# Gates' sums of the slot attention in pairs of token tiles, and a new table for the program's order

## The chip, the cores and the metric

The kernel runs on one core of a Trainium2 chip. The metric is the device time of one execution in microseconds (us), the median of several runs; lower is better.

## What is computed

Two sequences of 512 tokens, 128 features wide, pass through four layers. Each layer adds a gated attention on a context of 77 tokens and then a gated feed-forward part: (0) 16-head attention and a dense MLP, (1) multi-query attention and a mixture of 16 experts with two chosen and a shared expert, (2) attention and 32 experts with one chosen, (3) slot attention with a GRU cell, and an int8 matrix product. The part that the change touches is the slot attention of layer 3, three rounds of:

```python
for _ in range(3):
    sn = rmsnorm(slots, slot_norm_w)
    q = sn @ Wq.T
    attn = softmax(q @ k_proj.T * scale, axis=slots)      # over the 512 tokens
    attn = attn / (attn.sum(over the 77 keys) + EPS)
    updates = attn @ v_proj
    # GRU cell
    r = sigmoid(ir + hr);  z = sigmoid(iz + hz);  n = tanh(inn + r * hn)
    slots = (1 - z) * n + z * slots
```

Here (ir, iz, inn) comes from the updates through the input weights, (hr, hz, hn) from the slots through the hidden weights, each 3 x 128 wide.

## The kernel before

**Tiles.** The two sequences are called halves, h0 and h1 (`b` in the code). A half's 512 tokens are T = 4 tiles of 128 tokens. All activations stay on the chip.

**The order of the program.** The work is cut into steps named (phase, arguments). One step may have a piece on the matrix engine (PE), ScalarE (ACT), VectorE (DVE) and GpSimd (POOL). `half_steps` lists the steps of a half with a cost for each engine's piece and what it comes after; `schedule()` picks the steps one by one with a list scheduler whose ranks are shifted by the numbers in the table `LATER` (tenths of us, one for each piece of each half, and of the common preparations). What comes out is `ORDERS`, an order for each engine, in which that engine issues its instructions; engines wait for each other by semaphores. `schedule()` also deals the 8 PSUM banks and puts filler matmuls (128x512 on constants, their result is not read) where it expects PE to be idle.

**A round of slot attention** (`it` = 0, 1, 2) in a half:
- `square`: ACT squares and sums the slots (L1516, four ACTIVATEs), POOL makes the reciprocal root (L947, L948).
- `slots_turn`: PE transposes the slots (L1307), ACT copies them out of PSUM (L1382, tile q).
- `slot_products`: PE makes key products (8 matmuls), DVE scales them by the reciprocal root (L1843).
- `slot_scores`: PE transposes the products (L1332), DVE takes each key's maximum over the tokens (L1849), ACT the exponential (L1526).
- `hidden` 0, 1, 2: PE multiplies the slots by the hidden weights; ACT copies 0 and 1 (L1531), DVE scales and biases 2 (L1856).
- `slot_inverse`: DVE takes a reciprocal (L1865) and scales the values with it (L1866).
- `gru` 0 to 3: for each token tile PE makes one 386-column product into a bank of its own; DVE takes the reciprocal of its last column (L1877), and then multiplies by it and adds the hidden part (L1878, 384 columns, here called a tile's sum). The sum reads the reciprocal that DVE has just written, so `link` lets DVE wait for its own semaphore between the two: a hand-over.
- `gru_r`, `gru_z`, `gru_end`: ACT's tanh of the gates (L1537, L1541, L1542, L1547) and DVE's four products and sums of 512 columns and the product for z (L1884, L1885; L1890; L1894, L1895). After `gru_end` the slots are new.

After round 2: `slots_back` (L1901), and then for stage 7 `norm` (L1575, L1578, POOL L918), `norm_end` (L1584), `integers` (L1594 to L1596), `rounded` (L1602), PE's `turn` (L1074), its eviction (ACT L1382, DVE L1911), and `quantised`.

Of the rest, this is needed below: in the mixture of experts of layer 1, `gate` k and `up` k are pairs of products; ACT evicts a gate with Silu, DVE multiplies it with up. `gates1` is the choice of experts: DVE computes (L1757 to L1767), ACT takes an exponential and a tanh (L1487, L1488), and `weights_turn` continues on DVE (L1774 on).

```python
        step("gru", it, t, ... pe=0.65, dve=0.73)
    step("gru_r", it, after=[at("dve", "gru", it, T - 1)], act=0.53, dve=1.33)
```

Of the kernel before, what the change touches and what calls it, by code (L numbers as in the profile page):

```python
# [7 lines left out]
ALU = mybir.AluOpType  # L8
# [10 lines left out]
D = 128  # L19
# [122 lines left out]
def first_columns(name, k):  # L142
# [133 lines left out]
def half_steps(b, step):  # L276
# [108 lines left out]
    for it in range(ITERS):  # L385
# [13 lines left out]
        for t in range(T):  # L399
            step("gru", it, t, after=[at("dve", "slot_inverse", it)] + in_order("pe", "gru", it, t),  # L400
                 then={"dve": [at("act", "hidden", it, 1), at("dve", "hidden", it, 2)] + in_order("dve", "gru", it, t)},
                 pe=0.65, dve=0.73)
# [109 lines left out]
def units_of(phase, b, args):  # L512
# [37 lines left out]
    if phase in one:  # L550
        name, reader = one[phase]
        return [((name, *args[:1], b, *args[1:]), reader)]
    return {"project": [(("out", *args[:1], b), "dve")],
            "quantised": [(("out", 7, b), "dve")]}.get(phase, [])


def before_end(name):

    return BY_LANE[name[0]] * (LANES - 1 - name[-1]) if name[0] in BY_LANE else 0.0


def finished_by(phase, b, args):
# [11 lines left out]
    if phase == "choose":  # L574
        return units_of("hidden2", b, args)
# [1464 lines left out]
```

## Time and profile before

| | |
|---|---|
| median of 3 runs | 319.64 us (319.19 to 319.65) |
| the profiled execution's own time | 319.92 us |
| its span, first to last instruction | 318.1 us |
| PE busy | 301.1 us, 95% |
| DVE busy | 230.1 us, 72% |
| ACT busy | 144.1 us, 45% |
| POOL busy | 60.0 us, 19% |
| granted PE clock, mean | 0.999 |

The time outside the span is 319.92 - 318.1 = 1.8 us. Fillers count as busy PE. Busy times are sums over the whole program, whose parts have different limits; the rows below show the parts.

### The profile page before, as it was taken

Reading aid. Unit: us, or ns where it says so; the run is one execution under the profiler, and the core shown is the slowest. Engines: PE = TensorE matmul, PEld = TensorE weight load, DVE = VectorE, ACT = ScalarE, POOL = GpSimd, SP = SyncE. Lnnn points to the kernel's source line nnn. Section 1 sums busy time; section 2 is a strip of 40 time slices with the busy share of each in tenths; the row PEclk is TensorE's granted clock in tenths of the full one; section 3 lists DMA queues with packets and bytes.
Section 4 is the critical chain, followed back from the end, with each engine's and each line's share of the span. In section 5 each row is a group of like instructions: output and inputs, shape, how many; then the busy total and the mean of one; then the engine's idle time right before and its main releaser. Section 6 shows DMA issues by size and latency. Waiting matters only on the chain.

```text
span 318.1 us, 5708 instructions
## 1 busy us (share of the span) xinstructions
PE 301.1 (95%) x2106; PEld 200.6 (63%) x2106; DVE 230.1 (72%) x638; ACT 144.1 (45%) x300; POOL 60.0 (19%) x84
## 2 busy tenths in 40 slices
PE   8899989999899999999999999999999998999983
PEld 3463444794435668888788356589789774676431
DVE  4984885768966478988866495474548578899985
ACT  0458255232556771543305728413444635666311
POOL 6222454316001000103003301010210411011210
PEclk9999999999999999999999999999999999999999
DMA  7960220003100000000000000000000000000002
GB/s 181 300 221 0 68 66 14 0 3 99 47 0 2 2 0 0 3 0 0 2 0 2 1 3 2 0 2 0 0 2 0 2 1 0 2 1 2 0 1 66
DMA packets 8976, 8.73 MB, mean 27 GB/s; under 512 B 3547, under 2 KB 6901, under 8 KB 8949
## 3 DMA queue, kind: packets, MB, share of 16 engines
q1 hardware_dynamic: 8949, 8.37, 8.9%
q8 instruction: 17, 0.28, 0.4%
q14 instruction: 10, 0.08, 0.1%
HBM read 7.84 MB, written 0.52 MB: 26 GB/s over the span
## 4 chain that ended last, share of the span: by engine, by line
PE 73%; DVE 18%; ACT 5%; issue 2%; DVEq 0%; ACTq 0%
PE psum L980 67%; DVE mx L1715 5%; PE psum L1074 2%; DVE wide L1878 2%; ACT wide L1382 2%; ACT wide L1516 1%; DVE xn L1895 1%; PE psum L1112 1%; DVE wide L1885 1%; DVE xn_t L1894 1%; PE psum L1168 1%; DVE wide L1884 1%; PE psum L1160 1%; DVE xn L1584 1%; ACT q L1382 1%
## 5 line engine op out<-in xcount | busy, mean ns | idle before, releaser
L918 POOL TENSOR_TENSOR nw<-mv,minus_half 128x2 f32<-128x2 f32 x32 | 22.4, 714 | 130.1 <-DVE mv L1578 130.0
L1715 DVE TENSOR_REDUCE mx<-psum 128x4 f32<-128x308 f32 x96 | 38.5, 469 | 6.0 <-PE psum L980 5.9
L1382 ACT ACTIVATE wide<-psum 128x512 f32<-128x512 f32 x72 | 36.9, 612 | 11.9 <-PE psum L980 11.5
L1382 ACT ACTIVATE q<-psum 128x512 f32<-128x512 f32 (+1 forms) x36 | 21.2, 595 | 39.1 <-PE psum L980 31.4
L980 PE MATMUL psum<-q_hi,first_hi 128*128 128x512 f32 (+1 forms) x68 | 30.6, 451 | 0.0
L980 PE MATMUL psum<-wide 78*128 78x386 f32 (+1 forms) x71 | 26.0, 501 | 2.7 <-DVE wide L1866 1.5
L980 PE MATMUL psum<-halves 128*128 128x512 bf16 x110 | 27.0, 379 | 0.0
L980 PE MATMUL psum<-q_lo,first_hi 128*128 128x512 f32 (+1 forms) x68 | 26.9, 395 | 0.0
L980 PE MATMUL psum<-q_hi,first_lo 128*128 128x512 f32 (+1 forms) x68 | 26.8, 394 | 0.0
L980 PEld LDWEIGHTS psum<-early,wide 128*128 128x128 f32 x192 | 24.4, 191 | 2.3 <-ACT wide L1382 0.5
L980 PE MATMUL psum<-early,wide 128*128 128x128 f32 x192 | 24.9, 276 | 0.1
L980 PE MATMUL psum<-w_ffn,wide 128*128 128x128 f32 (+1 forms) x176 | 23.3, 277 | 0.0
L980 PEld LDWEIGHTS psum<-w_ffn,wide 128*128 128x128 f32 (+1 forms) x176 | 22.3, 192 | 1.5 <-issue 0.5
L980 PE MATMUL psum<-w_attn,q 128*128 128x128 f32 x176 | 22.8, 278 | 0.1
L980 PEld LDWEIGHTS psum<-w_attn,q 128*128 128x128 f32 x176 | 20.9, 192 | 1.3 <-ACT q L1382 0.6
L1584 DVE TENSOR_SCALAR xn<-x,mv,nw 128x128 f32<-128x128 f32 x64 | 19.0, 342 | 3.1 <-POOL nw L918 2.2
L980 PE MATMUL psum<-wide,heads_of 128*32 128x512 f32 x144 | 19.1, 601 | 0.3
L980 PE MATMUL psum<-wide,v_cols 128*32 128x512 f32 x144 | 19.0, 599 | 0.0
L1382 ACT ACTIVATE wide<-psum,cols 128x512 f32<-128x512 f32 x12 | 8.2, 685 | 23.4 <-PE psum L980 23.3
L980 PEld LDWEIGHTS psum<-wide 78*128 78x128 f32 (+1 forms) x71 | 11.2, 168 | 12.0 <-issue 4.4
L980 PEld LDWEIGHTS psum<-halves 128*128 128x128 bf16 x110 | 10.4, 98 | 11.8 <-issue 2.8
L1790 DVE TENSOR_TENSOR wide<-q,psum 128x512 f32<-128x512 f32 (+1 forms) x22 | 14.8, 682 | 3.3 <-PE psum L980 1.9
(232 smaller groups left out, 555.4 us busy)
## 6 DMA issues: line engine op xcount, KB each, us to landing
early<-in_ffn SPq DMA_DIRECT2D x8, 256.0 KB, 3.0
w_attn<-in_attn SPq DMA_DIRECT2D x1, 640.0 KB, 7.7
w_attn<-in_attn SPq DMA_DIRECT2D x2, 288.0 KB, 6.9
x<-in_x SPq DMA_DIRECT2D x2, 256.0 KB, 3.5
w_ffn<-in_ffn SPq DMA_DIRECT2D x1, 512.0 KB, 7.0
early<-in_ffn SPq DMA_DIRECT2D x1, 512.0 KB, 3.7
out<-x SPq DMA_DIRECT2D x2, 256.0 KB, 2.3
rows<-in_rows SPq DMA_DIRECT2D x1, 468.0 KB, 6.5
```

Source lines behind the costliest of these rows:

```text
L918: G.tensor_tensor(nw[:, b, 2, tiles], mv[:, b, tiles, 1], minus_half[:, tiles], ALU.pow)\
L980: return nc.tensor.matmul(out_, lhs, rhs, start=start, stop=stop, **kw)
L1074: last = nc.tensor.transpose(bk[:, t * P:(t + 1) * P], (y if stage == 7 else xn)[:, b, t, :], ident)
L1112: last = nc.tensor.transpose(bk[:, t * P:(t + 1) * P], mx[:, b, t, :], ident)
L1160: last = nc.tensor.transpose(bk[:, t * P:(t + 1) * P], sum_t[:, b, t * P:(t + 1) * P], ident)
L1168: last = nc.tensor.transpose(bk[:, t * P:(t + 1) * P], rinv_d[:, b, t, :], ident)
L1382: A.activation(dst, banks.bank(*name)[0:rows_, 0:cols_], fn, **kw).then_inc(drained["act"], 1)
L1516: last = A.activation(sq[:, b, t, :], slots[:, b, t, :], ACT.Square, accum_out=nw[:, b, 1, t:t + 1])
L1584: last = V.tensor_scalar(xn[:, b, t, :], x[:, b, t, :], mv[:, b, t, 0:1], nw[:, b, 2, t:t + 1], ALU.subtract, ALU.mult)
L1715: last = V.tensor_reduce(mx[:, b, t, lane_heads(g)], banks.bank("max", layer, b, t, g)[:, 0:GK].rearrange("p (h k) -> p h k", k=CTX), AX.X ...
L1790: V.tensor_tensor(wide[0:r, b, at_, :], act_s[k % 2][0:r, b, :], banks.bank("up", b, k)[0:r, :], ALU.mult)\
L1878: V.scalar_tensor_tensor(gates[:, b, t, :], u[:, 0:3 * D], inverse, gates_h[:, b, t, :], ALU.mult, ALU.add)\
```

## The change

1. `gru` keeps its four steps on PE. On DVE it becomes `gru_pair` 0 and 1: wait for the banks of two tiles, two reciprocals, one hand-over, two sums. No instruction is added or removed: 24 reciprocals and 24 sums stand in both kernels, 24 hand-overs become 12.
2. The costs in the scheduler's list follow (dve 1.25 for a pair in place of 0.73 for a tile).
3. `LATER` is replaced as a whole, so the order of all engines' steps is another. PE's steps are the same 352. The fillers are 117 in place of 120.

```diff
         for t in range(T):
-            step("gru", it, t, after=[at("dve", "slot_inverse", it)] + in_order("pe", "gru", it, t),
-                 then={"dve": [at("act", "hidden", it, 1), at("dve", "hidden", it, 2)] + in_order("dve", "gru", it, t)},
-                 pe=0.65, dve=0.73)
+            step("gru", it, t, after=[at("dve", "slot_inverse", it)] + in_order("pe", "gru", it, t), pe=0.65)
+        for i in range(T // 2):
+            step("gru_pair", it, i, after=[at("pe", "gru", it, 2 * i + 1), at("act", "hidden", it, 1), at("dve", "hidden", it, 2)]
+                 + in_order("dve", "gru_pair", it, i), dve=1.25)
...
-            def gru(b, it, t):
-
-                u = banks.bank("u", it, b, t)
-                inverse = route_s[:, b, 1, t:t + 1]
-                if t == 0:
+            def gru_pair(b, it, i):
+
+                def sums(t):
+                    return route_s[:, b, 1, t:t + 1]
+
+                if i == 0:
                     dve.wait_ge(*banks.emptied("hidden", it, b, 1))
                     dve.wait_ge(*banks.emptied("hidden", it, b, 2))
-                dve.wait_ge(*banks.full("u", it, b, t))
-                link(V.reciprocal(inverse, u[:, 3 * D:3 * D + 1]))
-                V.scalar_tensor_tensor(gates[:, b, t, :], u[:, 0:3 * D], inverse, gates_h[:, b, t, :], ALU.mult, ALU.add)\
-                 .then_inc(drained["dve"], 1)
+                for t in pair(i):
+                    dve.wait_ge(*banks.full("u", it, b, t))
+                    last = V.reciprocal(sums(t), banks.bank("u", it, b, t)[:, 3 * D:3 * D + 1])
+                link(last)
+                for t in pair(i):
+                    V.scalar_tensor_tensor(gates[:, b, t, :], banks.bank("u", it, b, t)[:, 0:3 * D], sums(t),
+                                           gates_h[:, b, t, :], ALU.mult, ALU.add).then_inc(drained["dve"], 1)
...
 LATER = {
-        0: (-720, -227, -147, -40, 24, -438, 82, 0, 148, 27, 0, 134, 356, -617, 127, -435, -86, -732, 484, -420, 638,
+        0: (868, 270, 915, -171, 978, 508, -72, 585, 984, 977, 981, 915, 740, 1006, 38, 111, 31, -341, 991, 398, 1020,
```

**Where the order changes, place 1.** DVE from the slots of round 0 to round 1, before. The first rows are the scaled products of h0 (round 1), the maximum, the hidden part and the products of h1 (round 0); then comes the inverse of h0, and after h1's inverse the tiles of h1 and, behind them, one tile of h0.

```order
L1843 TENSOR_TENSOR wide<-psum,nw 128x308
L1849 TENSOR_REDUCE nmax<-psum 77x1
L1856 SCALAR_TENSOR_TENSOR wide<-psum,hidden_bias 128x4x128
L1843 TENSOR_TENSOR wide<-psum,nw 128x308
L1865 RECIPROCAL nmax<-nmax 77x1
L1866 TENSOR_SCALAR wide<-vw,nmax 78x386
L1849 TENSOR_REDUCE nmax<-psum 77x1
L1865 RECIPROCAL nmax<-nmax 77x1
L1866 TENSOR_SCALAR wide<-vw,nmax 78x386
L1856 SCALAR_TENSOR_TENSOR wide<-psum,hidden_bias 128x4x128
L1877 RECIPROCAL route_s<-psum 128x1
L1878 SCALAR_TENSOR_TENSOR wide<-psum,route_s,wide 128x384
```

The same place of the change (the line numbers are 7 higher, from L1877 on 9 to 11 higher). First stand both halves' products:

```order
L1850 TENSOR_TENSOR wide<-psum,nw 128x308 x2
L1856 TENSOR_REDUCE nmax<-psum 77x1
L1872 RECIPROCAL nmax<-nmax 77x1
L1873 TENSOR_SCALAR wide<-vw,nmax 78x386
L1856 TENSOR_REDUCE nmax<-psum 77x1
L1863 SCALAR_TENSOR_TENSOR wide<-psum,hidden_bias 128x4x128
L1872 RECIPROCAL nmax<-nmax 77x1
L1873 TENSOR_SCALAR wide<-vw,nmax 78x386
L1886 RECIPROCAL route_s<-psum 128x1 x2
L1889 SCALAR_TENSOR_TENSOR wide<-psum,route_s,wide 128x384 x2
```

h0's maximum and inverse now come after h1's inverse, right ahead of h1's first pair. On PE the `hidden` 1 product of h0 moved ahead of h0's key products.

**Place 2.** DVE from h1's last tile of round 1 to h0's first tile of round 2, before:

```order
L1878 SCALAR_TENSOR_TENSOR wide<-psum,route_s,wide 128x384
L1843 TENSOR_TENSOR wide<-psum,nw 128x308
L1884 TENSOR_TENSOR wide<-wide 128x512
L1885 TENSOR_TENSOR wide<-wide 128x512
L1849 TENSOR_REDUCE nmax<-psum 77x1
L1890 TENSOR_TENSOR q<-wide,xn 128x512
L1856 SCALAR_TENSOR_TENSOR wide<-psum,hidden_bias 128x4x128
L1865 RECIPROCAL nmax<-nmax 77x1
L1866 TENSOR_SCALAR wide<-vw,nmax 78x386
```

and in the change:

```order
L1889 SCALAR_TENSOR_TENSOR wide<-psum,route_s,wide 128x384 x2
L1850 TENSOR_TENSOR wide<-psum,nw 128x308
L1856 TENSOR_REDUCE nmax<-psum 77x1
L1895 TENSOR_TENSOR wide<-wide 128x512
L1896 TENSOR_TENSOR wide<-wide 128x512
L1872 RECIPROCAL nmax<-nmax 77x1
L1873 TENSOR_SCALAR wide<-vw,nmax 78x386
L1901 TENSOR_TENSOR q<-wide,xn 128x512
L1863 SCALAR_TENSOR_TENSOR wide<-psum,hidden_bias 128x4x128
```

h0's maximum (L1849, now L1856) moved ahead of h1's two `gru_r` rows. On PE, h1's transposes still stand between the third and the fourth tile of h0's round 2.

## Rows read from the trace of the kernel before

**Rows 1.** The page: busy shares, and the chain by engine.
```profile
PE 301.1 (95%) x2106; PEld 200.6 (63%) x2106; DVE 230.1 (72%) x638; ACT 144.1 (45%) x300; POOL 60.0 (19%) x84
...
PE 73%; DVE 18%; ACT 5%; issue 2%; DVEq 0%; ACTq 0%
```

**Rows 2.** Busy us (x instructions) by stage; columns: stretch, length, engines, PE clock, DMA.
```profile
110.00:180.00 70.00, 69.98 (x466) 55.53 (x469) 54.46 (x149) 31.38 (x54) 9.20 (x10) 1.00 0.00 1
...
200.00:247.80 47.80, 47.80 (x335) 38.72 (x323) 28.23 (x72) 16.45 (x35) 4.46 (x7) 1.00 0.00 1
...
260.00:307.30 47.30, 43.31 (x232) 26.97 (x230) 43.42 (x107) 23.19 (x60) 6.71 (x10) 1.00 0.00 1
```

**Rows 3.** Timeline of DVE: tiles of h1, round 1; then two aggregates. Start us, length us.
```profile
276.46 0.16 DVE L1877 RECIPROCAL route_s<-psum 128x1 f32<-128x1 f32 x1
276.65 0.62 DVE L1878 SCALAR_TENSOR_TENSOR wide<-psum,route_s,wide 128x384 f32<-128x384 f32 x1
277.19 0.16 DVE L1877 RECIPROCAL route_s<-psum 128x1 f32<-128x1 f32 x1
...
305.63 0.26 DVE L1578 BATCH_NORM_AGGREGATE mv<-stats 128x2 f32<-128x9 f32 x2
```

**Rows 4.** The groups by line, DVE from 255 us: one aggregate alone.
```profile
L1578 DVE BATCH_NORM_AGGREGATE mv<-stats 128x2 f32<-128x9 f32 x8 | 1.1, 174 | 0.1
```

**Rows 5.** Timeline of ACT, before h1's round 0.
```profile
252.21 0.60 ACT L1531 ACTIVATE wide<-psum 128x512 f32<-128x512 f32 x1 [1.19 <-PE psum L980]
252.70 0.30 ACT L1516 ACTIVATE wide<-xn 128x128 f32<-128x128 f32 x1
...
253.87 0.58 ACT L1382 ACTIVATE q<-psum 128x512 f32<-128x512 f32 x1
```

**Rows 6.** Timeline of DVE, inverses and the first tile of h1's round 0.
```profile
250.94 1.28 DVE L1584 TENSOR_SCALAR xn<-x,mv,nw 128x128 f32<-128x128 f32 x4 [0.16 <-POOL nw L918]
...
256.11 0.15 DVE L1865 RECIPROCAL nmax<-nmax 77x1 f32<-77x1 f32 x1
...
257.09 0.69 DVE L1849 TENSOR_REDUCE nmax<-psum 77x1 f32<-77x512 f32 x1 [0.38 <-PE psum L1332]
258.69 0.16 DVE L1865 RECIPROCAL nmax<-nmax 77x1 f32<-77x1 f32 x1 [0.91 <-ACT wide L1526]
...
259.22 0.68 DVE L1856 SCALAR_TENSOR_TENSOR wide<-psum,hidden_bias 128x512 f32<-128x512 f32 x1
260.47 0.17 DVE L1877 RECIPROCAL route_s<-psum 128x1 f32<-128x1 f32 x1 [0.57 <-PE psum L980]
```

**Rows 7.** Timeline of DVE, h1's round 1 to h0's round 2.
```profile
279.60 0.48 DVE L1843 TENSOR_TENSOR wide<-psum,nw 128x308 f32<-128x308 f32 x1
280.15 0.69 DVE L1884 TENSOR_TENSOR wide<-wide 128x512 f32<-128x512 f32 x1
...
284.60 0.69 DVE L1895 TENSOR_TENSOR xn<-q,xn_t 128x512 f32<-128x512 f32 x1
...
287.63 0.62 DVE L1878 SCALAR_TENSOR_TENSOR wide<-psum,route_s,wide 128x384 f32<-128x384 f32 x1
288.64 0.48 DVE L1843 TENSOR_TENSOR wide<-psum,nw 128x308 f32<-128x308 f32 x1 [0.39 <-PE psum L980]
```

**Rows 8.** Timeline of PE, the same place: h0's four tiles with h1's transposes between.
```profile
284.11 2.18 PE L980 MATMUL psum<-wide 78*128 78x386 f32 x6
286.13 0.60 PE L1307 MATMUL psum<-consts,xn 128*128 128x128 f32 x4
286.57 0.81 PE L980 MATMUL psum<-wide 78*128 78x386 f32 x2
```

**Rows 9.** Timeline of PE: fillers, then h0's transposes of stage 7.
```profile
307.34 0.83 PE L1074 MATMUL psum<-consts,wide 128*128 128x128 f32 x4 [0.73 <-DVE wide L1602]
```

**Rows 10.** Timeline of ACT around the choice of experts, h0, layer 1.
```profile
111.80 1.28 ACT L1487 ACT_TABLE_LOAD   x1
...
116.61 1.28 ACT L1382 ACT_TABLE_LOAD   x1
```

More of the change, by code:

```diff
@@ L399, in half_steps @@
         for t in range(T):
-            step("gru", it, t, after=[at("dve", "slot_inverse", it)] + in_order("pe", "gru", it, t),
-                 then={"dve": [at("act", "hidden", it, 1), at("dve", "hidden", it, 2)] + in_order("dve", "gru", it, t)},
-                 pe=0.65, dve=0.73)
-        step("gru_r", it, after=[at("dve", "gru", it, T - 1)], act=0.53, dve=1.33)
-        step("gru_z", it, after=[at("dve", "gru", it, T - 1)], act=1.28, dve=0.6)
+            step("gru", it, t, after=[at("dve", "slot_inverse", it)] + in_order("pe", "gru", it, t), pe=0.65)
+        for i in range(T // 2):
+            step("gru_pair", it, i, after=[at("pe", "gru", it, 2 * i + 1), at("act", "hidden", it, 1), at("dve", "hidden", it, 2)]
+                 + in_order("dve", "gru_pair", it, i), dve=1.25)
+        step("gru_r", it, after=[at("dve", "gru_pair", it, T // 2 - 1)], act=0.53, dve=1.33)
+        step("gru_z", it, after=[at("dve", "gru_pair", it, T // 2 - 1)], act=1.28, dve=0.6)
         step("gru_end", it, after=[at("dve", "gru_r", it)], then={"dve": [at("dve", "gru_z", it)]}, act=0.53, dve=1.33)
@@ L554, in units_of, with pair @@
             "quantised": [(("out", 7, b), "dve")]}.get(phase, [])
+def pair(i):
+    return range(2 * i, 2 * i + 2)
 def before_end(name):
@@ L575, in finished_by @@
         return units_of("hidden2", b, args)
+    if phase == "gru_pair":
+        return [unit for t in pair(args[1]) for unit in units_of("gru", b, (args[0], t))]
     return units_of(phase, b, args)
@@ L1930, in _ @@
                     "choose": choose, "slot_products": slot_products, "slot_scores": slot_scores, "hidden": hidden,
-                    "slot_inverse": slot_inverse, "gru": gru, "gru_r": gru_r, "gru_z": gru_z, "gru_end": gru_end,
+                    "slot_inverse": slot_inverse, "gru_pair": gru_pair, "gru_r": gru_r, "gru_z": gru_z, "gru_end": gru_end,
                     "slots_back": slots_back,
```

84 rows, old and new, of the table LATER are left out of this document.

## The prediction

> **What bounds the kernel now.** The page first: PE is busy 95% of the span and carries 73% of the chain that ended last, DVE 18% [rows 1]. That average hides two stages, so the second view is busy time by stretch [rows 2]. From 110 to 180 us PE is busy 69.98 of 70 us, from 200 to 247.8 all of it: a change of order can win nothing there, only open a gap. From 260 to 307.3 us it turns round. There both halves go through the rounds of slot attention, DVE is busy 43.42 of 47.3 us, and PE's 43.31 holds most of the fillers. In that stretch DVE's order and work set the end; after it DVE hands the rounded tiles to PE at 307.34, which had waited 0.73 us for them [rows 9]. So I judge the change where `gru` stands, and check only that the rest doesn't get worse.
>
> The third view is DVE's timeline there. A tile is a reciprocal at 276.46, its sum at 276.65, the next reciprocal at 277.19 [rows 3]: 0.19 us from reciprocal to sum (the reciprocal itself is 0.16, so the hand-over shows as 0.03 to 0.04 and as the lost overlap), then 0.54 us to the next instruction although the sum lasts 0.62. A tile costs 0.73 us and 24 of them 17.5 us.
>
> **What a pair costs.** The two sums stay 0.54 us each, the second reciprocal still hands over in 0.19. Unknown is the distance between two reciprocals with no wait between them; no row has such a pair. The lower bound comes from the nearest small unlinked operation: two aggregates take 0.26 us together where one lasts 0.174, so the second starts 0.09 us behind the first [rows 3, 4]. The upper bound is 0.19, as if the hand-over were still there. I take 0.09, because that row is an unlinked one of nearly the same length. A pair is then 0.09 + 0.19 + 2 x 0.54 = 1.36 us against 1.46, and twelve pairs take 1.2 us off DVE (0 at the other bound). Nothing else is removed; PE issues the same steps.
>
> The Trainium skill speaks against this part. Its page "VectorE: DVE Perf Modes", section "The DRAIN you can't avoid", says that each Vector instruction waits for the pipe to empty and that leaving semaphores out of a chain saves nothing. The trace disagrees: in rows 3 a sum of 0.62 us is followed after 0.54 by an unlinked reciprocal, and the linked sum starts only after its reciprocal has ended. What the kernel would do by that rule is the third rival.
>
> **What the pair adds** is a wait. The first reciprocal now needs both tiles' banks. PE makes a tile in about 0.65 us (six matmuls, three tiles, take 2.18 with the pipeline's tail, two take 0.81) [rows 8]. Where DVE comes late, both are there and the wait costs nothing; where the second tile of a pair comes late, both sums stand behind it, and behind them ACT's tanh and the half's whole chain.
>
> **The walk through the last stretch.** I follow the new order with the durations of the old trace and compare the same step in both.
>
> (a) *Reaching h1's round 0: -0.4 us.* ACT copied `hidden` 1 of h0 at 252.21 and only then squared h1's slots at 252.70 [rows 5], though the slots were ready at 250.94 + 1.28 = 252.22 [rows 6]. PE now makes that product ahead of h0's key products, so ACT is free and squares at 252.26. The copy of the transposes follows PE's transposes and goes from 253.87 to about 253.5. All of h1's products, maximum and exponential move by that 0.4.
>
> (b) *h0's inverse ahead of h1's tiles: +0.9 us.* It ran at 256.11, in a gap, and cost nothing [rows 6]. Now DVE runs h1's inverse at 258.3 (258.69 - 0.4), which takes 259.22 - 258.69 = 0.53, then h0's maximum at 258.8. From a maximum to the reciprocal behind its exponential the rows have 258.69 - 257.09 = 1.6 us, of which the hidden part fills 0.6 [rows 6]. So h0's inverse starts at 260.4, ends at 260.95, and h1's first pair starts there, 0.5 after the 260.47 of before. -0.4 and +0.9 are that +0.5.
>
> (c) *Two pairs for four tiles: -0.2 us.* Both tiles are long there, so 2.72 in place of 2.92. h1's gates are out 0.3 us later than before, and this is carried through its `gru_end`, squares and products into round 1. h0's four tiles now all lie behind h1's `gru_end` (one stood in front of it before), but ACT's squares of h1 run beside them, and that is what h1 waits for.
>
> (d) *Place 2: +0.2 us.* After h1's tiles of round 1, DVE does h0's products at about the old 279.60, and then waits for PE to transpose them: the maximum can't start before some 1.3 us after the products, 0.9 idle. Before, `gru_r` of h1 came next after 0.55 us [rows 7]. h0's inverse gains 0.5 by this and h1's slots lose 0.7, to about 286.0 (284.60 + 0.69 before). PE's transposes of h1 come no later than before, since PE reaches them at 286.13 anyway [rows 8], 0.15 after the slots. So the fourth tile of h0 still ends at 287.4. Before, only its own sum was left, 287.63 + 0.62 = 288.25 [rows 7]. Now the third tile's sum has waited with it: 287.4 + 0.04 + 0.09 + 0.19 + 0.54 + 0.62 = 288.9, that is +0.6. DVE's products of h1, which ended an idle time of 0.39 at 288.64, start at 289.1, and h1's chain is 0.5 late, of which 0.3 was there.
>
> (e) *Last round: -0.2 us.* DVE is saturated from here to stage 7. The same instructions stand between h1's inverse and the rounding of h0, less two hand-overs: 2 x 0.1. `norm` of h0 moves ahead of h1's first pair and its POOL power is hidden by that pair; if it were not, 0.7 us more.
>
> Sum: -0.4 + 0.9 - 0.2 + 0.2 - 0.2 = **+0.3 us**. The 1.2 us that the pairs save do not add up on the path, since four of the twelve lie on it, 0.4 us, and the rest is given back in (b) and (d).
>
> **The rest of the order.** In the first 100 us PE's steps are the same but for two places, and its waits are for DVE's maxima, which stay. In layer 1 many gates and ups change places. PE's steps are the same, so the sum of its work is; I cost it at 0. Cover for DVE and ACT is PE's full queue, and the second rival is what it costs if that cover has a hole. Fillers fall from 120 to 117, all in idle time: 0.
>
> **Forecast: no change.** 319.92 + 0.3 = 320.2 us on the profiled execution, whose own time is 0.28 above the median, so **319.9 us** on the median of the runs. A measurement of this kernel can tell about 0.2% from no change, 0.64 us: it counts as the same. Chance 0.38.
>
> **Rival 1, faster: the freed DVE time reaches the end (0.32).** DVE has 3.9 us idle from 260 to 307.3 [rows 2], so the old order wasn't tight, and a new one can close some. My walk charges idle time at (b) and (d) by sums of hops of 0.03 to 0.15 us; if these waits are covered, the 1.2 of the pairs remain: 319.64 - 1.2 = 318.4, and with the gain of (a) and 0.1 of bounds 317.9. For it speaks that DVE is nearly full there, against it that PE's transposes pin the fourth tile.
>
> **Rival 2, slower: ACT's function tables stall layer 1 (0.22).** At h0's choice of experts ACT loads a table twice, 111.80 and 116.61, 1.28 us each [rows 10], and the scheduler's costs have 0.2 us for that step. It stood between gates 1 and 2, where PE had other work. Now it stands between gates 3 and 4: ACT can't start it before gate 3 is evicted, some 1.2 us later, and `weights_turn`, the projection of h1 and its LayerNorm stand behind it on DVE. PE needs that LayerNorm for the transposes of stage 3. By my count PE gets there 0.8 us before it is out, and loses another 0.4 at the second choice: 1.2 us on a PE that is full to the end of the stretch, 319.9 + 1.2 = 321.1; if both loads were bare, 2.6, beyond the range. It decides from the point at which PE reaches h1's stage-3 transposes before DVE's L1591 is done. Against it: PE idled 0.02 us there before [rows 2], and its queue has slack that I can't see.
>
> **Rival 3, the hand-over costs nothing (0.08).** A pair takes 1.46 us as two tiles did, so the change doesn't do what it says. (c) and (e) vanish: +0.7, 320.3 us, just on the slower side. By the skill's rule above this is the case; rows 3 make it unlikely.
>
> **Chances and range.** Faster 0.32, same 0.38, slower 0.22 + 0.08 = 0.30. The range reaches to 317.9 (rival 1 with its gains) and to 321.5 (rival 2 and the other bound of the pair, 321.1 + 0.4).
>
> **What would show it.** Right: pairs of 1.36 us, reciprocals 0.09 apart; DVE idle about 0.9 us before h0's maximum of round 2; h0's second pair of round 2 starting within 0.1 us of PE's tile; PE's transposes of stage 7 within 0.5 us of 307.34. Wrong: an idle PE between 110 and 180 us (rival 2), reciprocals 0.19 apart (rival 3), or DVE idle under 3 us from 260 to 307 with the end a microsecond earlier (rival 1).

## The result: 323.1 us, slower, and outside the range

The changed kernel takes 323.11 us (median of 4 runs, 322.55 to 323.36) against 319.41 us (4 runs, 319.19 to 319.65): a ratio of 1.0113, 95% interval 1.0095 to 1.0131. Forecast were 319.9 us and a range up to 321.5. The profiled execution of the changed kernel took 322.87 us with a span of 321.0 us.

The page of the changed kernel, against [rows 1]:

```profile
PE 299.7 (93%) x2103; PEld 199.6 (62%) x2103; DVE 228.9 (71%) x638; ACT 144.8 (45%) x300; POOL 60.3 (19%) x84
...
PE 68%; DVE 20%; ACT 6%; issue 2%; DMA 1%; SPq 1%; DVEq 0%; ACTq 0%
```

DVE did lose 1.2 us of work, yet PE's share of the chain fell from 73% to 68%: of the five points DVE took two, ACT one and the first loads (DMA and SPq) two, so the end hangs more on what PE waits for. The same stretches as in [rows 2], the last two 3 us longer, of the changed kernel:

```profile
110.00:180.00 70.00, 68.02 (x447) 55.48 (x451) 53.48 (x149) 29.45 (x49) 7.33 (x9) 1.00 0.00 1
200.00:250.80 50.80, 50.58 (x359) 39.96 (x359) 28.57 (x74) 19.15 (x41) 4.46 (x7) 1.00 0.01 1
260.00:310.40 50.40, 44.76 (x244) 28.46 (x243) 45.30 (x115) 25.82 (x66) 6.40 (x10) 1.00 0.00 1
```

PE, which was busy 69.98 of 70 us from 110 to 180, is idle for 2 us there. That is what the prediction named as the sign of rival 2. To see where all of it went I compare the start of the same PE step in both traces; the difference is how far the changed kernel lags. It starts 0.5 us ahead, and not because of the change: PE's first matmuls run without a wait in both, but here they keep their slow pace for a shorter time. Three such matmuls take 0.81 us a little later in both. The changed kernel, then the one before:

```profile
1.17 4.80 PE L987 MATMUL psum<-wide 128*128 128x512 bf16 x13 [1.17 <-DVE wide L1945]
1.17 5.67 PE L980 MATMUL psum<-wide 128*128 128x512 bf16 x13 [1.17 <-DVE wide L1934]
```

The profiled executions of all kernels differ by up to 0.9 us in this way before 20 us, so from here on only changes of the lag count.

| stretch (before) | lag at its start | at its end | cost |
|---|---|---|---|
| 71.0 to 78.5 us, layer 1, h1's transposes | -0.52 | +0.69 | 1.21 |
| 104.6 to 171.1, experts of layer 1 | +0.74 | +2.66 | 1.92 |
| 230.5 to 247.8, round 0 of h0 | +2.63 | +3.00 | 0.37 |
| 247.8 to 307.3, the stretch that the prediction walked | +3.00 | +3.08 | 0.08 |

**The first place.** The timelines of DVE and PE in the changed kernel, then POOL's:

```profile
75.78 1.79 DVE L1591 TENSOR_SCALAR xn<-x,mv,nw 128x128 f32<-128x128 f32 x2
...
78.11 0.41 PE L987 MATMUL psum<-keys_hi,q_hi 32*128 32x308 f32 x4 [1.41 <-DVE mx L1722]
...
75.00 2.49 POOL L944 TENSOR_TENSOR first_lo<-early,first_hi 128x512 fp32r<-128x512 f32 x2
```

and DVE and PE in the kernel before:

```profile
76.30 0.59 DVE L1584 TENSOR_SCALAR xn<-x,mv,nw 128x128 f32<-128x128 f32 x2
...
77.42 0.41 PE L980 MATMUL psum<-keys_hi,q_hi 32*128 32x308 f32 x4 [0.21 <-DVE mx L1715]
```

Two tiles that took 0.59 us take 1.79 us, and end at 77.57, just behind POOL's two subtractions (75.00 + 2.49 = 77.49); PE waits 1.41 us for the maxima behind them, where it waited 0.21. POOL's steps are `split` 4 and 5 of the weights, which the old order ran at 48.8 and 71.6 us.

**The second place.** ACT of the changed kernel:

```profile
116.43 0.60 ACT L1389 ACTIVATE q<-psum 128x512 f32<-128x512 f32 x1 [0.42 <-PE psum L987]
117.05 1.28 ACT L1494 ACT_TABLE_LOAD   x1
118.34 0.21 ACT L1494 ACTIVATE route_s<-route_s 128x4 f32<-128x4 f32 x1
...
122.83 1.28 ACT L1389 ACT_TABLE_LOAD   x1 [4.19 <-PE psum L987]
124.13 0.60 ACT L1389 ACTIVATE q<-psum 128x512 f32<-128x512 f32 x1
...
135.51 1.28 ACT L1389 ACT_TABLE_LOAD   x1 [1.08 <-PE psum L987]
136.81 1.09 ACT L1389 ACTIVATE q<-psum 128x512 f32<-128x512 f32 x2
```

and its PE:

```profile
124.78 0.66 PE L1081 MATMUL psum<-consts,xn 128*128 128x128 f32 x4 [0.89 <-ACT q L1389]
...
137.46 0.47 PE L987 MATMUL psum<-q_hi,first_hi 128*96 128x512 f32 x1 [1.09 <-ACT q L1389]
```

Here the Silu's table isn't loaded behind `gates1`, where ACT has 4.19 us with nothing to do, but after PE has finished gate 4 (of h0), 1.28 us in front of its eviction. PE's next step, h1's transposes of stage 3, is to go into the bank that gate 4 leaves. Before the change `gates1` stood between gates 1 and 2, so the second load stood in front of gate 2's eviction (116.61 + 1.28 = 117.89), and no step of PE was waiting for gate 2's bank [rows 10].

**The pairs** do what was expected of them, here DVE in round 1 of h0:

```profile
270.82 0.23 DVE L1886 RECIPROCAL route_s<-psum 128x1 f32<-128x1 f32 x2
271.08 1.14 DVE L1889 SCALAR_TENSOR_TENSOR wide<-psum,route_s,wide 128x384 f32<-128x384 f32 x2
272.14 0.23 DVE L1886 RECIPROCAL route_s<-psum 128x1 f32<-128x1 f32 x2
```

From pair to pair 1.32 us, where two tiles took 1.46 [rows 3]. The two reciprocals last 0.23 together, 0.16 each alone, so the second starts 0.07 to 0.08 behind the first. In round 0 of h0, the third row of the table, PE has not made the second tile when DVE asks for it, and DVE waits 0.60 us in the first pair and 0.33 in the second:

```profile
241.16 0.17 DVE L1886 RECIPROCAL route_s<-psum 128x1 f32<-128x1 f32 x1 [0.60 <-PE psum L987]
```

### The profile page after: what moved, and what is told of

It reads as the page before. It is cut to its first block, busy times and chain, and to the rows that moved or that the text cites. A ratio compares the mean times of both kernels' runs of the same rounds, so it can differ in the third digit from the quotient of the medians.

```text
span 321.0 us, 5703 instructions
## 1 busy us (share of the span) xinstructions
PE 299.7 (93%) x2103; PEld 199.6 (62%) x2103; DVE 228.9 (71%) x638; ACT 144.8 (45%) x300; POOL 60.3 (19%) x84
## 4 chain that ended last, share of the span: by engine, by line
PE 68%; DVE 20%; ACT 6%; issue 2%; DMA 1%; SPq 1%; DVEq 0%; ACTq 0%
PE psum L987 62%; DVE mx L1722 5%; PE psum L1081 2%; DVE wide L1889 2%; ACT wide L1389 2%; DVE wide L1896 1%; DVE wide L1895 1%; DMA early<-in_mask 1%; DVE xn L1591 1%; DVE nmax L1856 1%; DVE xn L1906 1%; ACT q L1389 1%; PE psum L1119 1%; DVE xn_t L1905 1%; ACT wide L1523 1%
## 5 line engine op out<-in xcount | busy, mean ns | idle before, releaser
L987 PE MATMUL psum<-q_hi,first_hi 128*128 128x512 f32 (+1 forms) x68 | 31.6, 465 | 1.1 <-ACT q L1389 1.1
L987 PE MATMUL psum<-wide 78*128 78x386 f32 (+1 forms) x71 | 25.2, 488 | 2.8 <-DVE wide L1873 1.6
L1591 DVE TENSOR_SCALAR xn<-x,mv,nw 128x128 f32<-128x128 f32 x64 | 20.3, 361 | 3.2 <-POOL nw L925 2.4
L944 POOL TENSOR_TENSOR first_lo<-early,first_hi 128x512 fp32r<-128x512 f32 (+1 forms) x9 | 10.7, 1198 | 34.4 <-ACT first_hi L1448 34.4
```

The source lines that it names most:

```text
L944: G.tensor_tensor(first_lo[:, lo:lo + n], raw(i), first_hi[:, lo:lo + n].bitcast(F32), ALU.subtract)\
L987: return nc.tensor.matmul(out_, lhs, rhs, start=start, stop=stop, **kw)
L1591: last = V.tensor_scalar(xn[:, b, t, :], x[:, b, t, :], mv[:, b, t, 0:1], nw[:, b, 2, t:t + 1], ALU.subtract, ALU.mult)
```

## The experiments

Theory: three parts of the new order cost 3.5 us between them, POOL's subtractions beside DVE (1.2), the table loads (1.9), and pairs where PE brings the tiles just in time (0.4 to 0.5); the pairs themselves are a gain elsewhere. Rivals: pairing as such is what costs, or one of the waits only hides another. Each kernel is compared with runs of the kernel before on the same chip (319.4 to 319.6 us).

Steps are moved with a helper that takes a step out of one engine's list in `ORDERS` and puts it behind another; the banks and all other lists stay.

**Loading the table early.**

```diff
                 A.activation(route_s[:, b, 7, :], lg[:, b, :, E1], ACT.Tanh, scale=0.5).then_inc(second_ready[b], 1)
+                A.activation(table_s[:, :], half_col[:, :], ACT.Silu)
```

> The changed kernel (323.1 us) with one more instruction: right behind each half's `gates1` ACT runs a Silu of one column into a scratch tensor, so that the function table is loaded there and not behind the wait of the next gate. Theory tables: the load of 1.28 us stood behind PE's gate 4 of h0 and gate 8 of h0, and PE's two idle times (0.89 at h1's stage-3 transposes, 1.09 at h1's gate 2) come from it. The second shrinks to about 0.2. The first falls to 0.6 and no further, since h1's xn is out only at 124.45, 0.3 before the transposes started: 0.3 + 0.9 = 1.2 off, 321.9 us; 1.8 off, 321.3, if the bank alone held the transposes. Rival: the idle times have another cause and only change their releaser, 323.1 us.

Measured: 321.27 us, ratio to before 1.0054 [1.0041, 1.0066], so 1.8 us less than the changed kernel. ACT now has this:

```profile
118.95 1.28 ACT L1497 ACT_TABLE_LOAD   x1
120.25 0.20 ACT L1497 ACTIVATE table_s<-half_col 128x1 f32<-128x1 f32 x1
123.11 0.60 ACT L1390 ACTIVATE q<-psum 128x512 f32<-128x512 f32 x1 [2.66 <-PE psum L988]
```

and PE has its transposes and gate 2 of h1 at these times:

```profile
123.99 1.12 PE L1082 MATMUL psum<-consts,xn 128*128 128x128 f32 x4
...
136.11 0.47 PE L988 MATMUL psum<-q_hi,first_hi 128*96 128x512 f32 x1
```

The idle time of 0.89 us is gone, and of the 1.09 some 0.1 is left. The first place gained 0.6: the transposes start 1.04 earlier (0.25 of lag taken off) but last 1.12 us instead of 0.66, since they now meet the tiles of h1's LayerNorm as they come out. The second gained 1.0. I had expected 0.3 and 0.9, and 321.3 us only if the bank alone held the transposes; the time is that one. So the theory of the tables holds. h1's LayerNorm is the next limit, as I had it, but a looser one: PE starts on its first tile and doesn't wait for the last.

**`gates1` of h0 back to an earlier place on ACT.**

```diff
+move("act", ("gates1", 0, ()), ("gate", 0, (1,)))
```

> The changed kernel (323.1 us), with only ACT's `gates1` of h0 moved from behind gate 3 to behind gate 1, near where it was before the change. Then the exponential's and the Silu's table are loaded while DVE has nothing for ACT, and h0's `weights_turn` and h1's LayerNorm on DVE come up to 1.3 us earlier as well. Theory tables: PE's idle time of 0.89 us at h1's transposes of stage 3 goes and the one of 1.09 at h1's gate 2 stays: 323.1 - 0.9 = 322.2 us. Rival: gate 2, now evicted 2.8 us later, holds up PE or DVE instead, 323.1 us or more.

Measured: 322.07 us, 1.0078 [1.0064, 1.0092]. Between the steps at 105.3 and 139.6 us of PE 0.84 us less are lost than in the changed kernel, and the idle time at h1's gate 2 is still 1.09 us. Both tables are loaded by 117.1 us:

```profile
114.24 1.28 ACT L1502 ACT_TABLE_LOAD   x1
...
115.85 1.28 ACT L1397 ACT_TABLE_LOAD   x1
117.15 1.08 ACT L1397 ACTIVATE q<-psum 96x512 f32<-96x512 f32 x2
```

Gate 2, evicted at 117.15 instead of 115.42, holds up DVE, though hardly PE. DVE waits as long for it as it waited for the exponential in the changed kernel; this run, then the changed kernel:

```profile
117.77 0.68 DVE L1805 TENSOR_TENSOR wide<-q,psum 96x512 f32<-96x512 f32 x1 [1.35 <-ACT q L1397]
...
118.68 0.17 DVE L1781 TENSOR_SCALAR route_s<-route_s 128x4 f32<-128x4 f32 x1 [1.35 <-ACT route_s L1495]
```

So h1's LayerNorm comes only 0.2 us earlier, not the up to 1.3 that I had expected, and PE's transposes again meet its tiles as they come out. That 0.2 is also what this run gains there beyond the early Silu's 0.6. The two loads are separate losses, and the place of `gates1` in the list is the cause of the first.

**Splits 4 and 5 at their old places.**

```diff
+move("act", ("split", 2, (4,)), ("scores", 1, (0, 1)))
+move("act", ("split", 2, (5,)), ("hidden0", 1, (3,)))
+move("pool", ("split", 2, (4,)), ("keys_in", 2, (2,)))
+move("pool", ("split", 2, (5,)), ("norm", 0, (2, 1)))
```

> The changed kernel (323.1 us), ACT's and POOL's splits 4 and 5 moved back to the places they had before the change (split 4 behind the first scores of layer 0, split 5 behind `hidden0` 3 of h1); all else stays. Theory clash: POOL's two splits from 75.0 to 77.5 stretched DVE's two xn tiles from 0.59 to 1.79 us and with them PE's idle time to 1.41 us; moved away, the pair lasts 0.6, the idle time falls to 0.2 and the time by 1.2 to 321.9 us. Rival: the tiles are slow for another reason, or the splits meet another DVE instruction on the path: 323.1 us within 0.3.

Measured: 321.71 us, 1.0068 [1.0056, 1.0081], 1.4 less than the changed kernel; the lag shrinks by 1.21 at that place and nowhere else. DVE and PE:

```profile
75.94 0.59 DVE L1602 TENSOR_SCALAR xn<-x,mv,nw 128x128 f32<-128x128 f32 x2
...
77.07 0.41 PE L998 MATMUL psum<-keys_hi,q_hi 32*128 32x308 f32 x4 [0.21 <-DVE mx L1733]
```

**ACT's two copies moved back alone.**

```diff
+move("act", ("split", 2, (4,)), ("scores", 1, (0, 1)))
+move("act", ("split", 2, (5,)), ("hidden0", 1, (3,)))
```

> The changed kernel (323.1 us) with ACT's copies for splits 4 and 5 back at their old places and POOL's subtractions left where the change put them (from 75.0 us). Theory clash with POOL: DVE's two xn tiles at 75.8 still take 1.8 us, 323.1 us within 0.3. Rival: ACT's copies or the wait for them are the cause, the tiles take 0.6 us and the kernel 321.7 us as with both moved back.

Measured: 322.92 us, 1.0105 [1.0090, 1.0121]. The pair of tiles still takes 1.79 us (at 76.02), PE still waits 1.41 us, the lag changes by nothing. POOL's subtraction is the cause, ACT's copy isn't.

**The same two splits put into the kernel before**, behind h1's norm of stage 2.

```diff
+move("act", ("split", 2, (4,)), ("query", 0, (1,)))
+move("act", ("split", 2, (5,)), ("split", 2, (4,)))
+move("pool", ("split", 2, (4,)), ("norm", 1, (2, 1)))
+move("pool", ("split", 2, (5,)), ("split", 2, (4,)))
```

> The kernel before (319.4 us) with splits 4 and 5 put, on ACT and POOL, where the changed order has them (behind h1's norm of stage 2). Theory clash: the two xn tiles of h1 at 76.3 are stretched from 0.6 to 1.8 us and PE waits for the maxima: 319.4 + 1.3 = 320.7 us. Rival: the clash needs something else of the new order, 319.4 us within 0.3.

Measured: 321.32 us, 1.0053 [1.0041, 1.0066]. At the same place PE waits 1.41 us and 1.21 us are lost, without any pair and with the old order of all else:

```profile
75.76 1.79 DVE L1595 TENSOR_SCALAR xn<-x,mv,nw 128x128 f32<-128x128 f32 x2
...
78.09 0.41 PE L991 MATMUL psum<-keys_hi,q_hi 32*128 32x308 f32 x4 [1.41 <-DVE mx L1726]
```

Another 0.84 us went from 78.5 to 94.5 us, which I had not expected. The trace shows what it was: the granted clock of PE falls to 0.50 there, its lower level of 1.2 GHz, and two matmuls of 128x512 at 81.10 take 2.08 us where they took 1.13. ACT's query and DVE, which waits 0.48 us for it at 83.94, come late behind them.

```profile
80.00:83.00 3.00, 2.82 (x9) 1.00 (x8) 3.00 (x9) 0.60 (x1) 0.97 (x1) 0.50 0.77 193
```

PE had been idle 1.41 us before it, but so it had in the changed kernel, whose clock stays at 1.00 in the same stretch. Why it fell is open. Only this execution has it: its mean clock is 0.993, that of the other four 1.000, and their median is 321.07 us, 1.55 more than the kernel before.

**Pairs in the old order.** The table of before, DVE's list with each two tiles replaced by a pair at the place of the second (and `gru_pair` as in the change).

```diff
+ORDERS["dve"] = [("gru_pair", b, (args[0], args[1] // 2)) if phase == "gru" else (phase, b, args)
+                 for phase, b, args in ORDERS["dve"] if phase != "gru" or args[1] % 2]
```

> The kernel before (319.4 us) with its own order, only that DVE takes the tiles in pairs (each pair at the place of its second tile). Theory: pairing itself is harmless, the loss of 3.7 us is all in the new order: twelve pairs at 0.14 us, of which four to six lie on the path, 319.4 - 0.6 = 318.8 us, range 318.2 to 319.4. Rival: sums that wait for the second tile's product cost more than the hand-overs save, as in the term of place 2 of the prediction: 319.4 + 0.6 = 320.0 us or more.

Measured: 320.63 us, 1.0037 [1.0025, 1.0050]: 1.3 us slower. The rival is right about the sign, and my theory that pairing is harmless falls. DVE in round 0 of h0:

```profile
239.72 0.16 DVE L1887 RECIPROCAL route_s<-psum 128x1 f32<-128x1 f32 x1
240.79 0.17 DVE L1887 RECIPROCAL route_s<-psum 128x1 f32<-128x1 f32 x1 [0.92 <-PE psum L988]
241.00 1.14 DVE L1890 SCALAR_TENSOR_TENSOR wide<-psum,route_s,wide 128x384 f32<-128x384 f32 x2
```

PE has the matmuls of the experts between the tiles there, so DVE gets them just in time, and the first sum waits 0.92 us for the second tile. By PE's transposes of h1 0.48 us are lost (247.8); 0.2 more in round 0 of h1, where DVE waits 0.38 for the second tile, and 0.5 in round 2, where three pairs wait 0.26 to 0.32 us each.

**Single tiles in the new order.** Inside `gru_pair`, for each tile a wait, a reciprocal, a hand-over and a sum:

```diff
                 for t in pair(i):
                     dve.wait_ge(*banks.full("u", it, b, t))
-                    last = V.reciprocal(sums(t), banks.bank("u", it, b, t)[:, 3 * D:3 * D + 1])
-                link(last)
-                for t in pair(i):
+                    link(V.reciprocal(sums(t), banks.bank("u", it, b, t)[:, 3 * D:3 * D + 1]))
```

> The changed kernel (323.1 us) with its order, but the pair undone inside its step: wait, reciprocal, hand-over, sum for each tile. Theory: the pair is worth 0.14 us where both tiles are there, some four to six of them on the path: 323.1 + 0.6 = 323.7 us. Rival: the wait for the second tile takes all of it back, 323.1 us or less.

Measured: 323.56 us, 1.0123 [1.0108, 1.0139]: the pairs gain 0.45 us in the new order (0.3 by the ratios, and the two intervals overlap; 0.5 in the traces). The traces show this to be two things. By 250.8 us single tiles are 0.48 ahead; from there to the end they lose 1.01. So in the new order pairs gain 1.0 us over the ten pairs of the last stretch and lose 0.5 with the two of round 0 of h0.

**Pairs only where both tiles had lain ready, in the old order.** Six pairs and twelve single tiles; as above, but a pair only for (round, half, pair) in

```diff
+TOGETHER = (0, 1, 1), (1, 0, 0), (1, 0, 1), (1, 1, 0), (1, 1, 1), (2, 1, 1)
```

> The kernel before (319.4 us) with its order; pairs only where both tiles lay ready in the trace before DVE came to them (second pair of round 0 of h1, all of round 1, second pair of round 2 of h1), the other twelve tiles one by one. Theory: six pairs at 0.14 us, about half of them on the path, 319.4 - 0.4 = 319.0 us, range 318.5 to 319.3. Rival: a pair is no gain in an order that was made for single tiles, 319.4 us or more.

Measured: 319.72 us, 1.0004 [0.9996, 1.0013]: no gain. Four of the six pairs are short, but DVE waits for what it has won: its products of h0 in round 2, which came at once at 279.60 before [rows 7], now wait 0.18 for PE, and those of h1 wait 0.39 as they did.

```profile
262.21 0.17 DVE L1889 RECIPROCAL route_s<-psum 128x1 f32<-128x1 f32 x1 [0.23 <-PE psum L990]
...
278.36 1.14 DVE L1892 SCALAR_TENSOR_TENSOR wide<-psum,route_s,wide 128x384 f32<-128x384 f32 x2
279.68 0.48 DVE L1853 TENSOR_TENSOR wide<-psum,nw 128x308 f32<-128x308 f32 x1 [0.18 <-PE psum L990]
...
288.73 0.48 DVE L1853 TENSOR_TENSOR wide<-psum,nw 128x308 f32<-128x308 f32 x1 [0.39 <-PE psum L990]
```

The other two pairs, the second of h1 in rounds 0 and 1, were not ready after all. A pair asks for its second tile some 0.6 us earlier than single tiles do, and DVE waits 0.23 us for it in the one and 0.14 in the other; the first costs PE 0.2 us. So this run doesn't show what pairs without any wait would be worth in the old order, and that a pair needs an order made for it is likely but not shown. The stretch from h1's transposes at 247.8 to PE's transposes of stage 7 lasts, by one trace each: old order and single tiles 59.5 us, old order and pairs throughout 60.3, new order and single tiles 60.6, new order and pairs 59.6.

**All three losses taken away at once:** the early Silu, the old places of splits 4 and 5, and single tiles in round 0 of h0 alone.

```diff
+                if (it, b) == (0, 0):
+                    together = [[t] for t in pair(i)]
```

> The changed kernel with three edits at once: the extra Silu of one column behind `gates1`, splits 4 and 5 at their old places, and the four tiles of round 0 of h0 one by one, the other twenty in pairs. Theory: the three losses are independent and are the whole loss: 323.1 - 1.8 - 1.4 - 0.5 = 319.4 us, range 319.0 to 319.8, the time of the kernel before. Rival: removing one only uncovers the next wait, 320 us or more.

Measured: 319.54 us (11 runs), 0.9997 [0.9988, 1.0005], as before. Within the interval of 0.4 us the three losses are the whole of it, and they add up.

**The same with all tiles in pairs**, that is without those last lines:

```diff
-                if (it, b) == (0, 0):
-                    together = [[t] for t in pair(i)]
```

> The kernel of the last call with the one-column Silu and the old places of splits 4 and 5, but with all twenty-four tiles in pairs, those of round 0 of h0 too. Theory: there the first sum of each pair waits for PE's second tile, and that costs 0.5 us as the trace with single tiles showed: 319.5 + 0.5 = 320.0 us. Rival: those waits were only visible beside the other stalls, 319.5 us.

Measured: 319.88 us, 1.0014 [1.0004, 1.0023]. Against the trace of the last kernel 0.49 us are lost between 233.6 and 247.6 and none behind; the medians differ by 0.3.

**Towards a faster kernel: splits 2 and 3.** The kernel before has the clash too, at a place that I had not looked at. Its DVE and POOL:

```profile
39.95 1.29 DVE L1724 COPY xn_t<-rinv 128x512 f32<-128x512 f32 x1
...
95.80 0.43 DVE L1724 COPY xn_t<-rinv 128x512 f32<-128x512 f32 x1
...
38.46 2.50 POOL L937 TENSOR_TENSOR first_lo<-early,first_hi 128x512 fp32r<-128x512 f32 x2 [4.55 <-ACT first_hi L1441]
```

PE is idle 0.76 us behind the long copy. First I tried this in the kernel with the three edits:

```diff
+move("act", ("split", 2, (2,)), ("slots_in", 2, (0,)))
+move("act", ("split", 2, (3,)), ("max_rows", 1, (0,)))
```

> As the kernel with the three edits (319.5 us), and ACT's split 2 ahead of `values` of h0, its split 3 behind `max_rows` of h1, so that POOL's two subtractions, now 38.2 to 40.7 us, no longer run beside DVE's copy at 39.69, which takes 1.29 us there where its like takes 0.43 to 0.55, with PE idle 0.99 behind it. Theory clash: the copy takes 0.43, PE's idle time falls to 0.15, 319.5 - 0.85 = 318.7 us, faster than both kernels. Rival: the copy is long for another reason, or split 3 stands in ACT's way ahead of h1's scores, 319.5 us or more.

Measured: 319.21 us, 0.9986 [0.9977, 0.9995]. The copy takes 0.43 us and PE's spread of the reciprocals comes 0.86 earlier; 0.28 of it is given back by 53.8 us. That is 0.35 us less than the kernel before, where 0.85 was forecast. Then in the kernel before, with nothing else changed:

```diff
+move("act", ("split", 2, (2,)), ("max_rows", 1, (0,)))
+move("act", ("split", 2, (3,)), ("split", 2, (2,)))
```

> The kernel before (319.5 us), single tiles and all, with only ACT's splits 2 and 3 moved behind `max_rows` of h1, so that POOL's two subtractions, now 38.46 to 40.96 us, come after DVE's copy at 39.95 (1.29 us there). Theory clash: the copy takes 0.43, PE's idle time of 1 us behind it falls to 0.15, some 0.3 of that is given back before the next stage as in the last run, 319.5 - 0.6 = 318.9 us, so the gain has nothing to do with pairs or the new order. Rival: the subtractions, now beside DVE's casts for the keys of layer 1, hold these up by more, 319.5 us or above.

Measured: 318.87 us (11 runs), 0.9981 [0.9972, 0.9990], the shortest time of all, though its interval overlaps that of the last kernel. DVE and POOL:

```profile
39.28 0.43 DVE L1733 COPY xn_t<-rinv 128x512 f32<-128x512 f32 x1
...
41.21 1.13 DVE L1637 CAST k_hi<-k_t 128x154 fp32r<-128x154 f32 x1
42.38 1.28 DVE L1638 TENSOR_TENSOR k_lo<-k_t,k_hi 128x154 fp32r<-128x154 f32 x1
...
45.59 0.32 DVE L1638 TENSOR_TENSOR k_lo<-k_t,k_hi 128x154 fp32r<-128x154 f32 x1
...
40.97 2.51 POOL L946 TENSOR_TENSOR first_lo<-early,first_hi 128x512 fp32r<-128x512 f32 x2 [7.73 <-ACT first_hi L1450]
```

The clash hasn't gone, it has moved: the cast and the first `k_lo` now pay, the latter 1.28 us where its like takes 0.32. But nobody waits for the keys of layer 1 there, and 0.55 us remain as a gain in the trace (0.7 in the medians).

## Why the prediction was wrong

**The step that failed** is "The rest of the order", with its "I cost it at 0". Of the 3.6 us that the lag grew by, 3.1 lie there (1.2 in the first 100 us, 1.9 in layer 1), 0.4 in round 0 of h0, which neither that paragraph nor the walk priced, and 0.1 in the walk. I argued from PE's sum of work and its full queue, which says what PE could do and not that the others bring it its inputs. Of a table that moves every list, each list had to be walked at each place where PE waits.

**POOL was not looked at at all.** The prediction had no term and no rival for its splits. [Rows 1] give POOL 19%, so it looked harmless; what counts is what DVE does meanwhile. The prediction says of PE that "its waits are for DVE's maxima, which stay"; one of them grew from 0.21 to 1.41 us, and PE's longest wait from 20 to 100 us, 0.76, was not for maxima at all, but for the copy at 39.95. The Trainium skill has the rule, in its page "SBUF — State Buffer", section "Who interferes with whom": GpSimd shares a pair of ports with VectorE; copies, casts and `tensor_scalar` in a two-port mode, and a `tensor_tensor` with both inputs in SBUF beside a GpSimd instruction that reads SBUF, can't run beside it, and whoever comes second waits until the other's instruction is over. The traces agree on each of these: the copy 1.29 us against 0.43, the `tensor_scalar` pair 1.79 against 0.59, the cast 1.13 against 0.23, `k_lo` 1.28 against 0.32, each ending 0.1 to 0.3 us after POOL's; while the maxima at 74.2 us, which read PSUM, kept their length (1.64 against 1.63). In which mode the copies and casts ran no trace says.

**Rival 2** was the right mechanism with the wrong size, 1.2 us for a measured 1.9. "0.8 at h1's stage-3 transposes" was 0.89 and "0.4 at the second choice" was 1.09. In the first, the reason was only half right: I made PE wait for DVE's L1591 behind a late `gates1`. What ended the wait was the bank of gate 4, behind the second load, which I hadn't placed; L1591 was out 0.3 us earlier and limits PE once the load is gone. In the second I left out that gate 8 empties the bank that h1's gate 2 needs. The chance of 0.22 was too low for a hole that the diff of ACT's list showed at two places.

**"What the pair adds"** named the wait for the second tile and then applied it at place 2 only. Round 0 of h0, outside the stretch that I walked, is where it cost 0.5 us.

**The walk** itself held step by step, its sum in part by luck (below). With h1's transposes at 247.81 and 250.81 as zero:

| step | forecast | measured |
|---|---|---|
| (a) h1's maximum of round 0 | -0.4 | -0.32 |
| (b) its first pair | +0.5 | +0.49 |
| (c) its last sum | +0.3 | +0.21 |
| (d) DVE's products of h1, round 2 | +0.5 | +0.31 |
| (e) PE's transposes of stage 7 | +0.3 | +0.08 |

The rows for (b) and (d), DVE of the changed kernel:

```profile
263.43 0.16 DVE L1872 RECIPROCAL nmax<-nmax 77x1 f32<-77x1 f32 x1 [0.25 <-ACT wide L1533]
...
263.96 0.22 DVE L1886 RECIPROCAL route_s<-psum 128x1 f32<-128x1 f32 x2
...
283.83 0.69 DVE L1856 TENSOR_REDUCE nmax<-psum 77x1 f32<-77x512 f32 x1 [0.82 <-PE psum L1339]
```

h0's inverse ran behind h1's and ahead of the pair, and DVE was idle 0.82 us before h0's maximum (0.9 forecast). Most of the difference of 0.2 at (e) is the size of the pair, 0.14 us saved instead of 0.10, at four pairs. What the sentence "four of the twelve lie on it, 0.4 us" missed is that the pairs are worth 1.0 us to this order: with single tiles it would have been 1.1 us slower than the old one, where my steps make it 0.7. Two errors, 0.4 too little for the order and 0.6 too little for the pairs, cancelled but for 0.2.

**Rival 3** falls: reciprocals 0.07 to 0.08 apart against the 0.16 that one lasts, and ten pairs worth 1.0 us. The rule of the Trainium skill that it rested on ("VectorE: DVE Perf Modes", section "The DRAIN you can't avoid"), that leaving out semaphores saves nothing, isn't borne out for instructions of one to 384 columns in this kernel. The prediction left out that the same section lets a next instruction that isn't held start earlier, and with that these traces agree. **Rival 1** falls by its own sign: DVE is idle 50.40 - 45.30 = 5.1 us in the stretch, where it asked for under 3. The time freed by the pairs did reach the end, 1.0 us of it, but the new order gave it away.

## What to carry to other kernels

When an order is searched anew against a cost model, look first at what the model doesn't price: function tables on ACT, and VectorE and GpSimd in each other's way. Lay the two lists of each engine beside the timeline of before and mark every table change and every long POOL instruction; each needs a place where nobody waits. Join two small instructions under one wait only where the second input is there by the time the first is taken, and expect a gain only if the work behind it is there as well.

## What was not expected of the hardware

- A table load stands on one side or the other of the wait of the instruction that it is for. At gate 0 it ran at 109.38, straight behind ACT's last work, and ACT idled after it (1.11 us); at gates 4 and 8 it ran after the idle time. At `gates1` of h1 in the kernel before it ran at 133.68, with 2.72 us idle behind it. Gate 0 and `gates1` have one semaphore to wait for, gates 4 and 8 two. That this decides it is only argued: no run changed the number of waits.
- A one-column Silu (0.20 us) moves the load to where it is written, and in the changed kernel is worth 1.8 us.
- DVE isn't slowed by POOL in proportion, it is stopped: the lengths of 1.1 to 1.3 us for work of 0.2 to 0.4 are what was left of POOL's instruction of 1.27 us, and 0.1 to 0.3 more. The copy started at 39.95, POOL's second subtraction ended at 40.96, the copy at 41.24.
- The same idle time of PE, 1.41 us at the same place, was followed by a fall of the granted clock to 0.50 for 3.4 us in one kernel's profiled execution and by none in the changed kernel's. Where two traces differ by more than a wait explains, look at the clock of the stretch.
